# Local attention weighed with v as the stationary operand, probabilities divided before they are turned, and a new order on five engines

## What is computed

```python
for i in range(6):
    x = attn_layer(shift_tokens(x), Wqkv[i], q_scale[i], k_scale[i], Wo[i]) + x
    x = ffn_layer(shift_tokens(x), ln_g[i], ln_b[i], W1[i], b1[i], W2[i], b2[i]) + x
```

```python
sim = jnp.einsum('bhwie,bhwje->bhwij', bq, bk2) * QK_SCALE
sim = jnp.where(mask, -jnp.finfo(sim.dtype).max, sim)
attn = jax.nn.softmax(sim, -1)
out = jnp.einsum('bhwij,bhwje->bhwie', attn, bv2)
```

## Time and profile before

| what | value |
|---|---|
| median of three executions | 1811.97 us (1806.33 to 1815.72) |
| the profiled execution, its own time | 1816.28 us |
| span of its trace | 1814.5 us |
| TensorE busy | 1625.9 us, 90% |
| VectorE busy | 1490.1 us, 82% |
| ScalarE busy | 1097.0 us, 60% |
| POOL busy | 1013.0 us, 56% |
| granted TensorE clock, mean | 0.955 of 2.4 GHz |

### The profile page before, as it was taken

One profiled execution on the slowest core, in us unless ns is written; L12 is line 12 of the kernel. 1 busy time (PEld: TensorE's weight loads), 2 busy tenths in 40 slices (PEclk: granted clock), 3 DMA queues, 4 the chain that ended last, 5 costly groups with the idle time before them and its releaser, 6 DMA issues. The chain is left out here.

```text
span 1814.5 us, 75400 instructions
## 1 busy us (share of the span) xinstructions
PE 1625.9 (90%) x31933; PEld 1249.7 (69%) x32029; DVE 1490.1 (82%) x3214; ACT 1097.0 (60%) x1971; POOL 1013.0 (56%) x932
## 2 busy tenths in 40 slices
PE   2547999989999989999989999989999989999975
PEld 1225777777777767777767777768777767777753
DVE  6859988888888788888888888888888888888841
ACT  2215666666766656666656666766667656767641
POOL 4416655585455485565585565585556575556510
PEclk8659999999999999999999999999999999999996
DMA  3011111111111121011111011111101111101101
GB/s 96 23 35 34 35 36 38 58 47 39 39 31 38 47 58 38 23 47 38 46 58 38 23 47 39 58 46 39 47 24 39 58 46 38 46 24 39 35 14 47
DMA packets 39012, 74.94 MB, mean 41 GB/s; under 512 B 8944, under 2 KB 19992, under 8 KB 38680
## 3 DMA queue, kind: packets, MB, share of 16 engines
q1 hardware_dynamic: 38680, 70.11, 13.1%
HBM read 20.08 MB, written 2.10 MB: 12 GB/s over the span
## 5 line engine op out<-in xcount | busy, mean ns | idle before, releaser
L662 POOL TENSOR_TENSOR qk<-qk,qk_sin 128x512 f32<-128x512 f32 x384 | 490.9, 1278 | 208.1 <-DVE qk_sin L736 208.1
L670 POOL TENSOR_TENSOR qk<-qk,rnorm 128x512 f32<-128x512 f32 x384 | 400.4, 1043 | 368.9 <-DVE rnorm L773 368.9
L913 ACT ACTIVATE squares<-bank 128x512 f32<-128x512 f32 x384 | 229.0, 596 | 167.7 <-DVE qk_sin L736 165.6
L1039 PE MATMUL bank<-w_hi,xs_hi 128*128 128x512 f32 x576 | 290.2, 504 | 13.1 <-ACT squares L913 7.7
L746 DVE TENSOR_REDUCE norm<-squares 128x8 f32<-128x512 f32 x384 | 258.5, 678 | 30.6 <-ACT squares L913 28.5
L730 DVE TENSOR_TENSOR qk<-bank,tables 128x512 f32<-128x512 f32 x384 | 261.8, 682 | 5.8 <-PE bank L1041 5.8
L736 DVE TENSOR_TENSOR qk_sin<-bank,tables 128x512 f32<-128x512 f32 x384 | 261.5, 681 | 0.0
L1049 PE MATMUL bank<-ident,qk 128*128 128x128 f32 x1536 | 236.5, 277 | 8.8 <-POOL qk L670 6.9
L1041 PE MATMUL bank<-w_hi,xs_lo 128*128 128x512 f32 x576 | 229.6, 399 | 1.2 <-issue 1.2
L1040 PE MATMUL bank<-w_lo,xs_hi 128*128 128x512 f32 x576 | 227.9, 396 | 0.8 <-issue 0.8
L1049 PEld LDWEIGHTS bank<-ident,qk 128*128 128x128 f32 x1536 | 184.6, 141 | 56.2 <-POOL qk L670 8.0
(11 more groups left out here) (139 smaller groups left out, 2629.5 us busy)
## 6 DMA issues: line engine op xcount, KB each, us to landing
v<-v SPq DMA_DIRECT2D x96, 390.0 KB, 3.5
v<-v SPq DMA_DIRECT2D x72, 130.0 KB, 3.4
w_raw<-in_L_ffn_Wqkv SPq DMA_DIRECT2D x36, 256.0 KB, 3.4
w_o_s<-in_L_ffn_Wo SPq DMA_DIRECT2D x6, 512.0 KB, 5.4
w_s<-in_L_ffn_W SPq DMA_DIRECT2D x6, 341.0 KB, 4.8
x_res_scratch<-mix_x_res SPq DMA_DIRECT2D x4, 256.0 KB, 2.4
f_x_res<-x_res_scratch SPq DMA_DIRECT2D x4, 256.0 KB, 3.6
out<-f_o_nat SPq DMA_DIRECT2D x4, 256.0 KB, 2.4
```

What stands on the lines that cost most here:

```text
L662: pool.tensor_tensor(qk[:, g % 2, c, :], qk[:, g % 2, c, :], qk_sin[:, c, :], ALU.add).then_inc(added[c], 1)
L670: pool.tensor_tensor(view, view, rnorm[:, g % 2, c * HPC:(c + 1) * HPC].unsqueeze(2) .to_broadcast([P, HPC, DH]), ALU.mult).then_inc(norme ...
L913: act.activation(squares[:, c % 2, :], bank_of(Q0 + c)[:], ACT.Square).then_inc(squared[c], 1)
L1039: pe.matmul(bank_of(c)[:], l_hi, w_hi[:, cols], start=True, stop=False)
```

## The change

`weigh` is one call with 64 matmuls. v is the stationary side (64 rows, 64 columns) and the turned probabilities move (32 columns). The result comes out with features on the partitions, as `merge_heads` needs it; `turn_o` and VectorE's `normalise` go, and `take_o` copies straight from the weighing's banks `wide`. Since the sum is no longer a column of the result, VectorE sums the exponentials (`sum_probs`, two reductions of 128x512, and `invert_sums`, one reciprocal of 128x16), and POOL multiplies the probabilities by the inverse (`scale_probs`, two operations of 128x512) before `turn_probs`. v loses its column of ones.

The order is new on every engine: the loops begin at step -1, q and k of block `step + 1` are projected in the step that projects v of block `step`, scores are made one step after and weighed in the step after that. The feed-forward pieces stand at other t: `shift_tail`, `centre` and `variance` at t = 2, `widen_rstd`, `scale_xn` and `expand` 0 at t = 3, `expand` 1 and 2 at t = 0. On ScalarE the three `gelu` now fall into three steps, with exponentials between. POOL splits two of the six weight chunks at t = 2 and four at t = 3, and their transfers start at t = 1 and t = 3 in place of 2 and 3.

```diff
-WEIGHT_ORDER = [4, 0, 1, 2, 3, 5]
+WEIGHT_ORDER = [0, 1, 3, 2, 4, 5]
...
+    Q0, Q1, K1, K0, V0, V1 = range(6)
...
+    BANK_OF = {V0: 0, Q0: 1, Q1: 0, V1: 1, K1: 0, K0: 1}
...
+            def scale_probs(g, r):
+                if not live(g):
+                    return
+                pool.wait_ge(row_inverted, g + 1)
+                view = probs[:, g % 2, r, :].rearrange("p (s k) -> p s k", k=2 * WINDOW)
+                pool.tensor_tensor(view, view, row_sum[:, g % 2, r, :].unsqueeze(2)
+                                   .to_broadcast([P, HPC, 2 * WINDOW]), ALU.mult).then_inc(probs_scaled[r], 1)
...
+                def split_weights(c, when):
+                    if before_layer and t == when:
                         weights.arrived(pool, layer, c)
-                        pool.wait_ge(projected[c], step + 1)
+                        pool.wait_ge(projected[c], NBLK * (item + 1))
                         weights.split(pool, layer, c)
...
-            def normalise(g, m):
-                if not live(g):
-                    return
-                sums = wide[:, :, 0:4 * (DH + 1)].rearrange("p w (s d) -> p w s d", d=DH + 1)
-                dve.wait_ge(weighed[m], 2 * (g + 1))
-                dve.reciprocal(row_sum[:, m, :, :].unsqueeze(3), sums[:, :, :, DH:DH + 1]).then_inc(inverted[m], 1)
-                dve.wait_ge(inverted[m], g + 1)
-                need(dve, o_turned[m], g)
-                dve.tensor_tensor(o[:, m, :, :, :], sums[:, :, :, 0:DH],
-                                  row_sum[:, m, :, :].unsqueeze(3).to_broadcast([P, 2, 4, DH]),
-                                  ALU.mult).then_inc(o_normed[m], 1)
+            def sum_probs(g, r):
+                if not live(g):
+                    return
+                dve.wait_ge(exp_done[r], g + 1)
+                need(dve, probs_scaled[1], g - 1)
+                dve.tensor_reduce(row_sum[:, g % 2, r, :], probs[:, g % 2, r, :].rearrange("p (s k) -> p s k", k=2 * WINDOW),
+                                  AX.X, ALU.add).then_inc(row_summed[r], 1)
+
+            def invert_sums(g):
+                if not live(g):
+                    return
+                dve.wait_ge(row_summed[0], g + 1)
+                dve.wait_ge(row_summed[1], g + 1)
+                dve.reciprocal(row_sum[:, g % 2, :, :], row_sum[:, g % 2, :, :]).then_inc(row_inverted, 1)
...
+                root(step)
                 residual(step - 3)
-                sum_squares(step, 1)
-                rotate(step, 3)
+                rotate(step + 1, 0)
+                rotate(step + 1, 1)
+                maximum(step - 1, 0)
+                maximum(step - 1, 1)
+                shift(step - 1, 0)
+                shift(step - 1, 1)
...
+                rotate(step + 1, 3)
+                sum_probs(step - 1, 0)
+                rotate(step + 1, 2)
...
+                sum_probs(step - 1, 1)
+                invert_sums(step - 1)
+                sum_squares(step + 1, 3)
...
-            def take_o(g, m):
-                if not live(g):
-                    return
-                act.wait_ge(o_turned[m], g + 1)
+            def take_o(g, w):
+                if not live(g):
+                    return
+                act.wait_ge(weighed, 4 * (g + 1))
                 need(act, wo_done, g - 1)
-                dst = o_t[:, g % 2, :, :].rearrange("p a (w m q) -> p w m a q", w=2, q=WINDOW)
-                act.copy(dst[:, :, m, :, :],
-                         bank[2 + m][:].rearrange("p (w a q) -> p w a q", w=2, q=WINDOW)).then_inc(o_taken[m], 1)
+                act.copy(o_t[:, g % 2, :, 2 * WINDOW * w:2 * WINDOW * (w + 1)],
+                         wide[:, w, :].rearrange("p (a q) -> p a q", q=2 * WINDOW)).then_inc(o_taken[w], 1)
...
+                square(step + 1, 1)
+                take_v(step, 1)
+                take_probs(step - 2, 1)
+                exponentiate(step - 1, 0)
+                take_probs(step - 2, 0)
+                if t == 3:
+                    bias_xn(item - 1)
+                exponentiate(step - 1, 1)
+                if t == 0:
                     gelu(item - 2, 1)
...
+                take_qk(step, 0)
+                take_qk(step, 3)
+                square(step + 1, 3)
                 if t == 3:
...
+                    gelu(item - 1, 0)
+                square(step + 1, 2)
...
-                if r == 0:
-                    need(pe, o_taken[0], g)
-                else:
-                    need(pe, qk_taken[3], g + 2, BLOCKS)
-                    if g + 2 > BLOCKS:
-                        need(pe, o_taken[1], g)
+                pe.wait_ge(probs_scaled[r], g + 1)
+                need(pe, qk_taken[2 if r == 0 else 1], g + 2, BLOCKS)
+                need(pe, p_taken[r], g)
...
-            def weigh(g, m):
+            def weigh(g):
                 if not live(g):
                     return
                 item, t = divmod(g, NBLK)
-                if m == 0:
-                    pe.wait_ge(p_taken[0], g + 1)
-                    pe.wait_ge(p_taken[1], g + 1)
-                    pe.wait_ge(v_moved[t], (16 if t == 0 else 32) * (item + 1))
-                    need(pe, o_normed[1], g)
-                else:
-                    pe.wait_ge(o_normed[0], g + 1)
+                pe.wait_ge(p_taken[0], g + 1)
+                pe.wait_ge(p_taken[1], g + 1)
+                pe.wait_ge(v_moved[t], (16 if t == 0 else 32) * (item + 1))
+                need(pe, o_taken[0], g)
+                need(pe, o_taken[1], g)
                 for s in range(2):
-                    for r in range(2):
-                        quad = 2 * s + r
-                        for h in range(4):
-                            for w in range(2):
-                                row = slice(2 * WINDOW * w, 2 * WINDOW * (w + 1))
-                                mm = pe.matmul(wide[WINDOW * h:WINDOW * (h + 1), w, quad * (DH + 1):(quad + 1) * (DH + 1)],
-                                               p_t[row, r, 2 * s + m, WINDOW * h:WINDOW * (h + 1)],
-                                               v[row, t, m, 8 * s + 2 * h + r, :], start=True, stop=True)
-                                if quad == 3 and h == 3:
-                                    mm.then_inc(weighed[m], 1)
-
-            def turn_o(g, m):
-                if not live(g):
-                    return
-                pe.wait_ge(o_normed[m], g + 1)
-                need(pe, qk_taken[m], g + 2, BLOCKS)
-                if g + 2 > BLOCKS:
-                    pe.wait_ge(p_taken[m], g + 1)
-                for w in range(2):
-                    for s in range(2):
-                        mm = pe.transpose(bank[2 + m][:, (2 * w + s) * P:(2 * w + s + 1) * P],
-                                          o[:, m, w, 2 * s:2 * s + 2, :].rearrange("p r d -> p (r d)"), ident[:])
-                mm.then_inc(o_turned[m], 1)
+                    for h in range(4):
+                        pair = 4 * s + h
+                        for m in range(2):
+                            for r in range(2):
+                                for w in range(2):
+                                    row = slice(2 * WINDOW * w, 2 * WINDOW * (w + 1))
+                                    col = (2 * pair + m) * WINDOW
+                                    mm = pe.matmul(wide[DH * r:DH * (r + 1), w, col:col + WINDOW],
+                                                   v[row, t, m, 2 * pair + r, :],
+                                                   p_t[row, r, 2 * s + m, WINDOW * h:WINDOW * (h + 1)],
+                                                   start=True, stop=True)
+                                    if pair == PAIRS - 1 and m == 1:
+                                        mm.then_inc(weighed, 1)
...
-            for step in range(STEPS):
+            for step in range(-1, STEPS):
                 item, t = divmod(step, NBLK)
                 project(step, V0)
-                project(step, Q0)
-                turn_qk(step - 2, 0, qk_taken[2], step - 1)
-                if t == 1:
-                    expand(item - 2, 2)
+                project(step + 1, Q0)
+                merge_heads(step - 3)
+                project(step + 1, Q1)
+                score(step - 1, step)
+                turn_probs(step - 2, 0)
+                project(step, V1)
+                turn_probs(step - 2, 1)
+                project(step + 1, K1)
                 if t == 3:
-                    centre(item - 1)
-                project(step, Q1)
+                    widen_rstd(item - 1)
+                project(step + 1, K0)
                 if t == 0:
-                    widen_rstd(item - 2)
-                weigh(step - 3, 1)
-                turn_o(step - 3, 0)
-                score(step - 2, step)
-                turn_o(step - 3, 1)
-                project(step, K0)
-                project(step, K1)
-                turn_qk(step - 1, 3, o_taken[1], step - 2)
-                merge_heads(step - 3)
+                    expand(item - 2, 1)
```

(23 more changed lines are left out.)

220 lines of the change are left out of this document (106 added, 114 removed).

## The result

The changed kernel takes 1894.92 us, median of four runs (1889.99 to 1900.16); the kernel before took 1813.85 beside it. The ratio is 1.044, 95% interval 1.041 to 1.047: slower by 4.4%, where 1757 and a gain were forecast. The change is slower, not faster, and the time lies above the range.

What follows compares the result with a forecast made beforehand. TensorE, busy for 95% of the stretch between first and last score, was taken as the bound. -79 + 33 - 30 + 16 + 5 = -55 took the profiled 1816.28 to 1761; the median, 4 lower, gave 1757 us, range 1715 to 1830.

Steps and rivals of the forecast that it cites:

- Turns of `o`, -79: On TensorE, two turns of `o` per block at 0.41 us each go away: 79 us less.
- the weighing, +33: On TensorE, the new burst of 128 records lasts 1.92 us against 1.58 in two before: 33 us more.
- the rival of load and stream in turn: Weighing tiles do not load while they stream, a burst lasts 2.7 to 2.9 us: 1825 us, chance 0.22.
- the scores' pace: Rival: the weighing burst runs as fast as the scores, 1.42 us: 1730 us, 1693 without stalls; chance 0.15.
- Layer ends, -30: Of 45 us lost, mostly at the five layer ends, 15 remain after POOL's splits and `root` are moved.
- Instruction supply, +16: Instruction stalls inside TensorE's new weighing burst, 40 times 0.4 us: 16 us more; ends 0 and +37.
- Off the path, 0: Work added on VectorE, POOL (200 us of products) and ScalarE (60 us) costs nothing, covered by TensorE's 16 us step.
- The chain of waits: From output product through `residual`, VectorE and ScalarE to `turn_qk` and `weigh`: 6.3 us, beside 6.3 of TensorE's work.
- The slack is a few tenths: In the worst step, the tightest chain behind `residual` has a few tenths of slack against TensorE's work.
- the new order waits: Rival: late hops in the chain, or a late `gelu(0)`, cost 0.5 to 1 us a step: 1805 to 1853; chance 0.15.
- Ends, +5: Pipeline start with a step -1 of four chunks costs between 0 and one step (16 us), taken as 5.
- The test that I had named: Wrong if steps keep 16.8 us while TensorE's parts are shorter: then an engine other than TensorE sets the step.

Runs made afterwards that it cites:

- e12: Kernel before, old order and two weighing bursts, each matmul in the new form with the four tiles visited in turn: 1847.7 us, 1.018.
- e10: Changed kernel, GpSimd scaling after `root`, maximum before `root` left out, second head of each pair left out of the weighing: 1782.12 us, 0.982 of the kernel before.
- e1: Changed kernel, with GpSimd waiting for `root` before it scales both halves of the probabilities, then normalising: 1860.34 us, 1.026 of the kernel before.
- e2: Changed kernel, `root` without its maximum and with its guess as a two-source `scalar_tensor_tensor` instead of `tensor_scalar`: 1875.95 us, 1.035 of the kernel before.
- e9: Kernel before, with a useless 128x1024 product put on GpSimd beside `root`: 1846.1 us, 1.017.
- e6: Changed kernel, GpSimd scaling after `root`, no maximum before `root`, weighing and score bursts each cut into two of 64 records: 1857.32 us, 1.022 of the kernel before.

## Why the prediction was wrong

The forecast against what was measured, term by term:

- **Turns of `o`, -79, and the weighing, +33.** Right in kind and nearly in size. Taking the 15th percentile of the distances between output products for each t, four undisturbed steps took 63.95 us before and 62.44 after: 36 us less over 24 items, where 46 were forecast. The burst is 2.00, not 1.92, 8 us more. Its cause is sharper than I had it: 0.058 a record on each tile, beside 0.055 for the load alone. So the rival of load and stream in turn (2.7 or more) did not come, nor did the scores' pace.
- **The Trainium skill's page "TensorEngine Tiling (Array Packing)"**, section Performance Considerations, advises against taking tiles from a dimension that is already small. The burst did get longer, 2.00 against 1.58 in two, which fits the advice; the runs give as its cause the pace of one tile. The overhead of some 60 cycles that the page gives each matmul (25 ns at 2.4 GHz, an estimate from it) no run shows between tiles: 64 records take 1.07 us in e12, 17 ns each, and before they took 0.79, 12 ns each.
- **Layer ends, -30.** Too high. Waits for `rnorm` fell from 17.2 us to 2.0, and 3.7 for `w_lo` came: about -12 by the waits. By the distance between items nothing was gained: the one across a layer end was 7.9 us longer than the others before (73.4 against 65.5) and 7.3 after (76.2 against 68.8). I had also put the late `root` down to POOL's splits being long; its own instructions were held up by them, as the lines above show. And 0.69 + 1.29 is 1.98 for a split, not 1.9.
- **Instruction supply, +16.** The mechanism was right, the size was not. I counted stalls inside the weighing at 0.4 us. Measured as distances of over 0.5 us between starts inside a burst, there are 25 of 1.54 us in the weighing, and 29 of 1.80 in the scores; before, 2 of 1.1 and 37 of 1.19. 46 us became 91. So this term, too, failed in its size. The supply is no slower: from the start of the last packet on the instruction queue to TensorE's next record pass 2.5 us before and 2.4 after. But before, some 198 records (median, weight loads counted too) still began in that time, now 127 in the scores and 148 in the weighing: TensorE runs dry sooner, and why is not shown. With the half clock behind the stalls and the waits of others, e10 puts the weighing's share at up to 69 us, though half of the instructions went with it.
- **Off the path, 0.** This is the step whose mechanism failed. "I cost all three at nothing; their cover is TensorE's step" took an engine's work as a sum and not as a place. The 200 us on GpSimd stretched `root` on VectorE by 74 us (e1, e2, e9 show the lock), and `residual`, mask and scores stand behind `root`: 35 us. TensorE, named as the cover, was busy for 89% of the stretch, not 94% or more.
- **The chain of waits.** "The slack is a few tenths" was right, and so every delay on VectorE cost half of itself: 69 gave 35, 21 gave 10, and in the old kernel 60 cost 25. The rival "the new order waits", 1805 to 1853, foresaw late hops behind `residual` and late work of ScalarE, not a longer `root` ahead of it, and 1895 lies outside even it.
- **Ends, +5.** The first scores start at 158.65 us, 158.35 before, and 60.5 us follow the start of the last ones, 62.2 before: about -1.

Sum: 35 (lock) + 53 (supply, 69 less the 16) + 8 (burst) + 18 to 30 (layer ends) - 6 (ends) = 108 to 120 of the 138 us between 1757 and 1895. The 69 is an upper bound, so at least 18 us are open. The test that I had named came true: steps were not shorter while TensorE's parts were. What stays open, too, is why a stall in the scores grew from 1.19 to 1.80 us in the new order; it was not tried apart from the weighing.

## What to carry to other kernels

Before moving work to GpSimd, lay it beside VectorE's instructions in time. In these kernels a `tensor_scalar` on SBUF, or an instruction with two sources there, lasted until GpSimd's instruction ended, with few exceptions, and a sum of busy times doesn't show it. Look for it in the trace at hand: short instructions of VectorE that last longer at some places than at others. Let the tiles of a dense burst of small matmuls come in turn. Cutting a burst of 256 instructions in two took away most of its stalls in the weighing, but the cut gained 10 us there and lost 16 in the scores, so it has to be tried. A pipeline that has no slack pays for the delay of an engine at 85% though another is the busiest.

## What the runs showed of the hardware

- An instruction of 128x32 or 128x36 on VectorE that lasts 0.17 to 0.20 us alone took 0.54 to 1.17 in the timelines shown where GpSimd was at work, and ended 0.03 to 0.05 after GpSimd's. Of `root`'s instructions that began at least 0.25 before GpSimd's ended, 175 of 182 ended within 0.08 of them in the changed kernel, and 48 of 48 before. An instruction of 128x512 with one source in a bank kept its 0.68.
- A 64x64 tile took an fp32 record each 0.058 us in a burst on four tiles, and no slower or faster on two (e10), so half of the records on half of the tiles took just as long as all: 1.99 against 2.00.
- The order in which the same 64 records visited four tiles moved the burst from 1.07 to 1.39 us.
- Where stalls were shorter the clock was higher: stretches at 1.2 GHz (158 to 1752 us), 89 us in the changed kernel, were 14 in e6, the mean clock of the whole execution 0.945 and 0.964.
